# A fixed slot tile for each expert, overflow tiles, and 64 KB weight blocks whose down matrix is cut in column halves

## The reference

```python
x = x + _L0_ffn_ref(_layernorm(x), ...)        # twice
# NUM_EXPERTS = 160, TOP_K = 8, HIDDEN = 128, INTER = 64, T = 4096 tokens
probs = jax.nn.sigmoid(x @ router_w.T + expert_bias[None, :])
top_w, top_idx = jax.lax.top_k(probs, TOP_K)
top_w = top_w / (jnp.sum(top_w, axis=-1, keepdims=True) + 1e-09) * ROUTED_SCALE
h1 = jax.nn.silu(jnp.einsum('th,eih->eti', x, w_gate))
routed = jnp.einsum('eti,ehi->th', h1 * combine.T[:, :, None], w_down)   # combine: top_w at top_idx
shared = jax.nn.silu(x @ w_gate_shared.T) @ w_down_shared.T
```

## Time and profile before

| | |
|---|---|
| time, median of 3 runs | 2897.25 us (2891.38 to 2900.32) |
| the profiled execution, its own time | 2902.76 us, its span 2900.9 us |
| mean granted TensorE clock | 0.723 of full speed |
| busy: PE, DVE, ACT, POOL | 1753.3, 1334.2, 970.8, 1057.4 us |
| expert stages, about | 447 to 930 us (run 0) and 1319 to 1801 us (run 1) |

### The profile page before, as it was taken

How to read it: one execution, slowest core, us unless ns; L and a number is a source line. 1 busy time by engine, 2 the same in 40 slices (tenths; PEclk the granted TensorE clock), 3 DMA queues, 4 the chain that set the end, 5 groups by cost and what they waited for, 6 DMA issues and landing times.

```text
span 2900.9 us, 44112 instructions
## 1 busy us (share of the span) xinstructions
PE 1753.3 (60%) x13716; PEld 1146.8 (40%) x13716; DVE 1334.2 (46%) x3558; ACT 970.8 (33%) x1719; POOL 1057.4 (36%) x1177
## 2 busy tenths in 40 slices
PE   3765506776666454556776676422325488888975
PEld 2544404555444242244554454100124234455443
DVE  3648811222334677473222333543215466666644
ACT  3651102232223321312232222356761123444342
POOL 2001777724651774757714651771000200000000
PEclk9985557778878655557788787655555568998985
DMA  8941118999997111117999997120000000000001
GB/s 234 382 181 29 51 53 275 325 304 292 321 289 241 52 52 54 52 55 244 327 308 294 310 301 241 51 54 8 4 2 0 0 1 1 1 1 2 1 1 29
DMA packets 332506, 393.39 MB, mean 136 GB/s; under 512 B 57952, under 2 KB 222512, under 8 KB 332208
## 3 DMA queue, kind: packets, MB, share of 16 engines
q1 hardware_dynamic: 215616, 171.43, 19.0%
q10 hardware_dynamic: 83984, 153.13, 15.4%
q0 software_dynamic: 32768, 67.17, 7.7%
HBM read 242.13 MB, written 164.63 MB: 140 GB/s over the span
## 4 chain that ended last, share of the span: by engine, by line
PE 36%; DVE 15%; DMA 13%; ACT 11%; issue 10%; SPq 9%; POOL 6%; DVEq 0%; ACTq 0%; POOLq 0%
DMA arena<-expert_blocks 12%; SPq L1819 6%; ACT arena L955 5%; PE psum L1918 4%; PE psum L1909 4%; POOL slot_rows L1725 4%; PE psum L448 3%; SPq L1815 3%; PE psum L1347 2%; PE psum L1900 2%; PE psum L1328 2%; PE psum L432 2%; PE psum L993 1%; PE psum L427 1%; ACT arena L1210 1%
## 5 line engine op out<-in xcount | busy, mean ns | idle before, releaser
L1736 POOL DMA_INDIRECT arena<-slot_results,SLOTS x512 | 490.7, 958 | 503.1 <-DMA slot_results<-arena 285.8
L1725 POOL DMA_INDIRECT slot_rows<-arena,SLOTS x512 | 493.4, 964 | 309.4 <-issue 308.8
L1699 DVE COPY arena<-psum 128x512 f32<-128x512 f32 x288 | 198.6, 690 | 742.3 <-PE psum L1918 719.4
L1909 PE MATMUL psum<-arena 128*64 128x128 f32 x2304 | 236.5, 336 | 278.4 <-DMA arena<-expert_blocks 271.0
L1779 ACT ACTIVATE arena<-psum 128x512 f32<-128x512 f32 x288 | 171.9, 597 | 476.4 <-PE psum L1900 467.6
L1909 PEld LDWEIGHTS psum<-arena 128*64 128x64 f32 x2304 | 154.5, 165 | 349.0 <-issue 291.5
L169 POOL TENSOR_SCALAR rstd<-mv 128x4 f32<-128x4 f32 x32 | 6.2, 193 | 772.3 <-DVE mv L577 771.8
L1900 PE MATMUL psum<-ident,arena 128*128 128x128 f32 x1152 | 231.6, 335 | 84.9 <-DMA arena<-slot_rows 84.3
L1918 PE MATMUL psum<-arena 64*128 64x128 f32 x2304 | 253.3, 350 | 0.0
L1786 ACT ACTIVATE arena<-psum 128x256 f32<-128x256 f32 x288 | 110.4, 383 | 338.5 <-PE psum L1909 335.3
L1918 PEld LDWEIGHTS psum<-arena 64*128 64x128 f32 x2304 | 189.6, 230 | 64.4 <-issue 64.2
(11 more groups left out here) (234 smaller groups left out, 3064.5 us busy)
## 6 DMA issues: line engine op xcount, KB each, us to landing
arena<-expert_blocks SPq DMA_DIRECT2D x1152, 96.0 KB
arena<-slot_rows ACTq DMA_DIRECT2D x288, 256.0 KB
slot_results<-arena ACTq DMA_DIRECT2D x288, 256.0 KB
slot_rows<-zeros SPq DMA_DIRECT2D x2, 18432.0 KB, 84.2
slot_rows<-arena,SLOTS POOLq DMA_INDIRECT x512, 2.2
arena<-slot_results,SLOTS POOLq DMA_INDIRECT x512
expert_blocks<-in_expert_w SPq DMA_DIRECT2D x1, 7680.0 KB, 26.0
expert_blocks<-in_expert_w SPq DMA_DIRECT2D x1, 5120.0 KB, 52.7
```

The source lines that it names most:

```text
L1699: dve.tensor_copy(YSB[:, p].rearrange("p (c h) d -> p h c d", h=2), psum[:, first:first + 2, 0:256].rearrange("p h (c d) -> p h c d", c=2) ...
L1725: pool.indirect_dma_start(out=slot_rows[h], out_offset=bass.IndirectOffsetOnAxis(ap=SLOTS[:, t, k:k + 1], axis=0), in_=XNH[:, t], in_offse ...
L1736: pool.indirect_dma_start(out=GATHERED[:, t % TPI, k], out_offset=None, in_=slot_results[h], in_offset=bass.IndirectOffsetOnAxis(ap=SLOTS[ ...
L1909: mm = pe.matmul(psum[lo:lo + INTER, 2 + 5 * (p % 2), o:o + P], EWB[:, p, q, 0:INTER], XSBT[:, p, P * q:P * q + P], start=True, stop=True, ...
```

## The change

- **Slot tiles.** Tile e of the 288 now belongs to expert e for its first 128 tokens; the other 128 tiles take what is over, sorted by expert (`DELTA`, `MORE_GROUPS` = 32 groups). The 40 groups of own tiles (`OWN_GROUPS`) have experts that are known when the kernel is written, and the two kinds are interleaved (`GROUP_ORDER`).
- **Placing.** `FIRST` is replaced by the constant `OWN`. `rows_of_slots` takes four token tiles together: it compares with the end of the own tile, adds `DELTA` where a number is past it, runs one sum over 640 numbers so that the eight numbers of a token come out in order, multiplies by `MASK`, takes four times the eight largest and subtracts neighbours.
- **Weights.** A block is 64 KB: 128 partitions x 128 numbers. The down matrix's first 64 output columns lie in partitions 0 to 63 and the others in 64 to 127. `expert_blocks` is laid out by partition, so a partition's row is 80 KB long and holds all experts. For an own group SP issues four DMAs, each with 32 partitions and rows of 2 KB (four experts side by side); for an overflow group four DMAs with rows of 512 B, by expert numbers that it reads as before. SP's loop is written out.
- **Down products.** The gated rows of a slot tile stand in one partition half, but half of its down matrix in the other. DVE copies them across (`in_both_halves`, two copies of 64 x 256), and PE makes eight products of 64 columns where it made four of 128; the last four wait for the copies.

```diff
-        EW = INTER + D
+        OWN_GROUPS = NE // GROUP
+        MORE_GROUPS = GROUPS - OWN_GROUPS
+        GROUP_ORDER = sorted(range(GROUPS), key=lambda n: (n + 0.5) / OWN_GROUPS if n < OWN_GROUPS else (n - OWN_GROUPS + 0.5) / MORE_GROUPS)
+        EW = INTER + D // 2
-        expert_blocks = nc.dram_tensor("expert_blocks", (NE * P, EW), F32).ap()
+        expert_blocks = nc.dram_tensor("expert_blocks", (P, NE * EW), F32).ap()
...
-            dve.wait_ge(s_slotm.sem, s_slotm.at(run, t))
-            stand(dve)
-            dve.max(S8[:, j], SLOTM[:, j]).then_inc(s_s8.sem, 1)
...
+            dve.tensor_tensor(OVER, SLOTM, every(OWN_END), ALU.is_gt).then_inc(link.sem, link.one())
+            dve.wait_ge(link.sem, link.so_far())
+            dve.tensor_tensor(OVER, OVER, every(DELTA), ALU.mult).then_inc(link.sem, link.one())
+            dve.wait_ge(link.sem, link.so_far())
+            dve.tensor_tensor(OVER, SLOTM, OVER, ALU.add).then_inc(link.sem, link.one())
+            dve.wait_ge(link.sem, link.so_far())
+            stand(dve)
+            dve.tensor_tensor_scan(PLACED.rearrange("p t e -> p (t e)"), ones_row[:, 0:1].broadcast_to([P, TPI * NE]), OVER.rearrange("p t e -> p (t e)"),
+                                   0.0, ALU.mult, ALU.add).then_inc(link.sem, link.one())
+            dve.wait_ge(link.sem, link.so_far())
+            dve.tensor_tensor(PLACED, PLACED, MASK[:, TPI * i:TPI * i + TPI, :], ALU.mult).then_inc(link.sem, link.one())
+            for j in range(TPI):
+                last = TOPK * (TPI - 1 - j)
+                dve.max(S8[:, last:last + TOPK], PLACED[:, j]).then_inc(link.sem, link.one())
...
+        def in_both_halves(dve, run, h, g):
+            hr = HALVES * run + h
+            dve.wait_ge(c_he.sem, c_he.at(hr, 0, g + 1))
+            dve.tensor_copy(HEB[INTER:, g % 2, 2:4], HEB[0:INTER, g % 2, 0:2]).then_inc(c_both.sem, 1)
+            dve.tensor_copy(HEB[0:INTER, g % 2, 2:4], HEB[INTER:, g % 2, 0:2]).then_inc(c_both.sem, 1)
...
+            def own_weights(n, p):
+                for part in range(GROUP):
+                    rows = slice(P // GROUP * part, P // GROUP * (part + 1))
+                    sp.dma_start(EWB[rows, p].rearrange("p q c -> p (q c)"), expert_blocks[rows, GROUP * EW * n:GROUP * EW * (n + 1)]).then_inc(c_ew[p].sem, 16)
+            def more_weights(n, p):
...
-                    sp.dma_start(EWB[:, p, q], expert_blocks[bass.ds(e * P, P), :]).then_inc(c_ew[p].sem, 16)
+                    sp.dma_start(EWB[:, p, q], expert_blocks[:, bass.ds(e * EW, EW)]).then_inc(c_ew[p].sem, 16)
...
-            pe.wait_ge(o_link.sem, o_link.at(run, h))
-            pe.matmul(psum[:, 7, 0:NE], ident[:], FIRST, start=True, stop=True, skip_group_check=True)
+            pe.wait_ge(o_own, 3)
+            pe.matmul(psum[:, 7, 0:NE], ident[:], OWN, start=True, stop=True, skip_group_check=True)
...
-                for q in range(GROUP):
-                    c, lo = P * (q // 2), INTER * (q % 2)
-                    mm = pe.matmul(psum[:, 3 + 2 * (p % 2) + q % 2, c:c + P], HEB[lo:lo + INTER, p % 2, c:c + P],
-                                   EWB[lo:lo + INTER, p, q, INTER:EW], start=True, stop=True, skip_group_check=True, tile_position=(lo, 0))
+                for other in range(2):
+                    if other:
+                        pe.wait_ge(c_both.sem, c_both.at(hr, g, 2 * p + 2))
+                    for c in range(GROUP // 2):
+                        for half in range(2):
+                            q, lo = 2 * c + (half ^ other), INTER * half
+                            mm = pe.matmul(psum[:, 3 + 2 * (p % 2) + half, INTER * q:INTER * q + D // 2], HEB[lo:lo + INTER, p % 2, 2 * other + c],
+                                           EWB[lo:lo + INTER, p, q, INTER:], start=True, stop=True, skip_group_check=True, tile_position=(lo, 0))
...
             for run in range(HALVES):
+                in_both_halves(dve, run, 0, 0)
                 for g in range(GROUPS):
+                    if g + 1 < GROUPS:
+                        in_both_halves(dve, run, 0, g + 1)
                     results_out(dve, run, 0, g)
...
-            sp.dma_start(block_of[:, 0:INTER], whole[:, 0:INTER]).then_inc(blocked, 16)
-            sp.dma_start(block_of[:, INTER:, 0:INTER], whole[:, INTER:, 0:INTER]).then_inc(blocked, 16)
-            sp.dma_start(block_of[:, INTER:, INTER:], whole[:, 0:INTER, INTER:]).then_inc(blocked, 16)
+            sp.dma_start(block_of[:, :, 0:INTER], whole[:, :, 0:INTER]).then_inc(blocked, 16)
+            for half in range(2):
+                sp.dma_start(block_of[INTER * half:INTER * half + INTER, :, INTER:], whole[0:INTER, :, INTER + D // 2 * half:INTER + D // 2 * (half + 1)]).then_inc(blocked, 16)
```

More of the change, by code:

```diff
@@ L1493, in program @@
         INCL = view([P, NE])
-        FIRST = view([P, NE])
+        OWN_END = view([P, NE])
+        OWN = view([P, NE])
+        DELTA = view([P, NE])
+        OVER = view([P, TPI, NE])
+        PLACED = view([P, TPI, NE])
         JUNK2 = view([P, GROUP, NE], BF16)
@@ L1687, in rows_of_slots @@
[L1687 to L1691 removed]
+            link = Order(s_slot, run, i)
@@ new lines, in rows_of_slots @@
+            every = lambda row: row.unsqueeze(1).broadcast_to([P, TPI, NE])
+            dve.wait_ge(s_slotm.sem, s_slotm.at(run, TPI * i + TPI - 1))
+            dve.tensor_tensor(OVER, SLOTM, every(OWN_END), ALU.is_gt).then_inc(link.sem, link.one())
[3 more added lines that the diff above has]
+            dve.tensor_tensor(OVER, SLOTM, OVER, ALU.add).then_inc(link.sem, link.one())
@@ new lines, in rows_of_slots @@
+            stand(dve)
+            for j in range(TPI):
+                last = TOPK * (TPI - 1 - j)
+                dve.max(S8[:, last:last + TOPK], PLACED[:, j]).then_inc(link.sem, link.one())
+            dve.wait_ge(link.sem, link.so_far())
+            dve.scalar_tensor_tensor(SLOT[:].rearrange("p t k -> p (t k)"), S8[:, 0:TPI * TOPK], -1.0, S8[:, 1:TPI * TOPK + 1],
+                                     ALU.add, ALU.subtract).then_inc(link.sem, link.one())
+            dve.wait_ge(link.sem, link.so_far())
@@ L1812, in experts_sync @@
             hr = HALVES * run + h
[L1814 removed]
+            def own_weights(n, p):
[3 more added lines that the diff above has]
+            def more_weights(n, p):
+                stand(sp)
                 _, experts = nc.values_load_multi_w_load_instructions(
[L1816 removed]
+                    EXPERT[0:1, h, n, :], engines=[sp.engine], min_val=0, max_val=NE - 1,
                     skip_runtime_bounds_check_because="EXPERT counts at most NE experts and is clamped to NE - 1 where it is made")
                 for q, e in zip(range(GROUP), experts):
[L1819 removed]
+                    sp.dma_start(EWB[:, p, q], expert_blocks[:, bass.ds(e * EW, EW)]).then_inc(c_ew[p].sem, 16)
             sp.wait_ge(o_expert.sem, o_expert.at(run, h))
[L1822 to L1831 removed]
+            for g in range(GROUPS):
+                n, p = GROUP_ORDER[g], g % UNROLL
+                if hr or g >= UNROLL:
+                    sp.wait_ge(c_y.sem, c_y.at(hr, 0, g - UNROLL + 1))
+                if n < OWN_GROUPS:
+                    own_weights(n, p)
+                else:
+                    more_weights(n - OWN_GROUPS, p)
         LOGITS = (6, 2)
@@ L1947, in middle_vector @@
             dve.memset(C9[:], 0.0)
+            dve.memset(S8[:], 0.0)
+            own_tiles(dve)
             for h in range(HALVES):
```

88 lines of the change are left out of this document (47 added, 41 removed).

## The result

The change takes 3136.04 us (median of 4 runs, 3123.36 to 3145.66) against 2894.32 us for the kernel before on the same chip: the ratio is 1.083, 95% interval 1.079 to 1.088. It is slower by 8%, where 2823 us was forecast with a range of 2780 to 2905. The execution shown here took 3138.0 us, 235.2 us more than the one of before.

A forecast was written before the change was run, and what follows sets the result against it. The DMA engines were taken to bound the expert stages beside POOL, with SP as close without it. From 2902.8 us, minus 118 for weights plus 44 for placing gave 2829, less 5.5 for the median: 2823 us, range 2780 to 2905.

The forecast's parts named there:

- TensorE at the full clock fits under the first and sets the second: Expert stages: TensorE's 2.47 us a group fits under DMA's 2.81 beside POOL and sets the pace without POOL (DMA 2.35).
- rival 1: Expert stages: TensorE bounds at half clock; with the clock mix as granted 3.09 and 2.79 us a group, 2884 us; chance 0.14.
- The weights' price: Expert-stage weight DMAs: 0.91 us a group against 1.32, 0.41 us less, 118 us less over 288 groups.
- The overflow rows: Weight DMAs of an overflow group: 512 rows of 512 B cost 0.99 us, between 0.88 and 1.32.
- the own rows: Weight DMAs of an own group: 128 rows of 2 KB cost 0.85 us, between 0.72 and 1.43.
- The placing: Added DVE passes in `rows_of_slots`: 6.1 us a call, 16 calls, 44 us in sum on the path.
- the calls under the dispatch: Placing calls before the first expert stage, after the first call, lying under POOL's dispatch: they cost nothing.
- the calls between the stages: Placing calls between the first and second expert stage: 6.1, 12.8 and 18.3 us on the path.
- Rival 2: Own groups' weight loads: 32-partition DMAs pay double, 1.43 us; 25 us saved, placing's 44 stay, 2916 us; chance 0.12.
- Rival 3: Weight loads: 512 B rows, blocks 80 KB apart, cost what 768 B cost; 1.06 us a group, 2865 us; chance 0.10.
- Rival 4: Expert stages: DVE's copies hold up POOL, its pace 1.26 us becoming 1.78; 2946 us; chance 0.06.

The follow-up runs named there:

- wide_again: The changed kernel with each down product streaming 128 columns instead of 64, the extra results unread; 2890.25 us, ratio 0.998 to the kernel before.
- wide96: The changed kernel with each down product streaming 96 columns instead of 64; 2932.49 us, ratio 1.012 to the kernel before.
- half_columns: The kernel before with its four down products cut to 64 columns, leaving out half of the output; 2903.31 us, ratio 1.002.
- small_blocks: The kernel before with 64 KB blocks laid out by partition, copies across and eight 128-column down products, slots and placing as before; 2880.18 us, ratio 0.995.
- parity_again: The changed kernel without split or copies: four 128-column products, own groups 64 KB a DMA packed by parity, overflow groups 96 KB; 2908.75 us, ratio 1.004.
- wide_spread: The changed kernel with 128-column down products and the eight adds of `sum_rows` two a group instead of eight at each fourth; 2893.51 us, ratio 0.999.
- the alone-run: The kernel before plus only the change's added placing passes, on tiles that nothing reads; 2939.9 us, ratio 1.014.
- parity_span: parity_again with an own group loaded by one DMA over 128 partitions instead of four over 32 each; 2910.0 us, ratio 1.005.

## Why the prediction was wrong

**The step that failed** is the one that let TensorE pass: "TensorE at the full clock fits under the first and sets the second", and in rival 1 the condition "if the clock stays as granted". The prediction priced TensorE at 2.47 us a group at the full clock and 4.40 at half; measured are 2.21 and 4.00, both a tenth less. It then took for the forecast that the full clock holds, and for rival 1 that the mix stays as granted (0.77, 0.87), which gave 2884 us and a chance of 0.14. No case had a clock that falls because of the change. It fell to 0.50, and 4.00 us against 3.35 and 3.34 before (483.0 and 481.1 us over 144 groups) is the 192 us that the stages lost. The argument against rival 1, that it would be the busy engine then, was the wrong one: busy for 106.00 of 106.00 us it stayed low. `wide_again`, `wide96` and `half_columns` show that the columns streamed behind each weight load decide it in this loop, in both directions. Whether the columns of each pass count, or those streamed over a stretch of time, no run separates.

**The weights' price nearly held.** SP's queue in the changed kernel, 500 to 580 us:

```profile
q1 hardware_dynamic: 7303, 5.25, 25.0%
...
arena<-expert_blocks SPq DMA_DIRECT2D x81, 64.0 KB
```

That is 0.250 x 80 / 20.25 = 0.99 us a group, against 0.91 forecast and 1.32 before: a saving of 0.33 us a group and not 0.41. The overflow rows were priced a little too high (0.92 us in `small_blocks` against 0.99), so by the mean of 0.99 the own rows cost (72 x 0.99 - 32 x 0.92) / 40 = 1.05 us, an estimate, against 0.85. `parity_again` gives less for them: 33.2% of 80 us without 11.25 overflow groups at 1.32 leaves 0.84 us for each of its 14 own groups, so their price stays open between the two. With the clock up (`wide_again`: 32.1% with 104 DMAs, or 0.99) the two stages save 32.6 and 47.0 us, 80 in all where 118 were forecast; and that execution took 2871.31 us, 19 less than the median of its kernel, so 80 is rather too much. Groups there take 3.13 and 3.01 us, not 2.8 and 2.5. What holds them at that is not settled; it is not the length of DVE's sums (`wide_spread`). TensorE still waits 77.4 and 74.9 us for weights in the two stages (132.7 and 138.3 before), while SP waits 93.6 and 83.1 us for TensorE to free one of the four weight buffers (50.2 and 50.7 before). That the four buffers are too few is a rival that no run tested.

**The placing held in its sum, but partly by luck.** 44 us were forecast and the alone-run gives 41. A call in the changed kernel (DVE, start and us):

```profile
277.47 0.82 DVE L1704 TENSOR_TENSOR arena<-arena 128x640 f32<-128x640 f32 x1
...
280.16 1.49 DVE L1711 TENSOR_TENSOR_SCAN arena<-ones_row,arena 128x640 f32<-128x640 f32 x1
281.69 0.82 DVE L1714 TENSOR_TENSOR arena<-arena 128x640 f32<-128x640 f32 x1
282.66 1.01 DVE L1719 MAX8 S<-arena 128x8 f32<-128x160 f32 x4
```

The pieces are nearly as priced (4 x 0.825, 1.6, 1.0), and the first dispatch begins at 285.77, 5.3 us later instead of 6.1. But the stage begins 15.0 later: POOL took (457.10 - 285.77) - (442.05 - 280.46) = 9.7 us more for its first 128 starts, and a term for that was missing: the prediction put the calls under the dispatch at nothing. 21 of these 128 DMAs stand beside DVE passes over 640 numbers and take 1.07 to 2.13 us, together 10.4 us more than at 0.96 us each; before, four did, for 0.7 us (rows in the last section). In the alone-run the same stage begins 16.7 us later where 6.1 were forecast, the calls between the stages cost 33.6 where 37.2 were, and the two stages are 9.3 us shorter than before, for which nothing was forecast. The sum is right since these errors cancel.

**Rival 2** (32-partition DMAs at double price) fell: `parity_span` and `parity_again` differ by 0.1%. The Trainium skill's rule that partitions 0 to 31 reach half of the ports ("SBUF — State Buffer", Door 1: The DMA port swizzle) is not contradicted by that, since other transfers to all partitions ran beside; no run here shows it alone. **Rival 3** (512 B rows at the price of 768 B) fell: it needs 1.32 us for a group of 512 B rows 80 KB apart, and `small_blocks`, where all groups are such, measures 0.92. (The changed kernel's 0.99 alone would not decide it, since it lies halfway between the forecast's 0.91 and the rival's 1.06.) **Rival 4** (copies hold up POOL) fell for the copies: with them POOL makes 84 DMAs in 106 us in the changed kernel's first window as against 83. It holds in a small way for the placing passes, which the prediction had not considered there.

## What to carry to other kernels

When an edit splits TensorE's passes, price the new loop at both clock levels and ask whether it still fits under the next limit at the lower one; a granted clock read before the edit is no property of the stretch and may fall with it. Few streamed columns behind each weight load is the sign to look for, and streaming columns that nobody needs can be the faster choice (3133 to 2890 us here, which only brings the time back to that of before). Where two limits are as close as DMA and SP here, an edit that relieves one is worth only the distance to the other.

## What the runs showed of the hardware

- TensorE, busy without a pause, stayed at 1.2 GHz (0.50) from 480 to 742 us and in most of the rest of stages of 574 and 582 us with passes of 64 columns, and came back to 2.4 GHz only at the starts of three halves, for less than 12 us each; the same weight loads with 96 columns were granted 0.89 and 0.74, with 128 columns 0.98 and 0.90, in the same windows.
- A pass of 64 columns is hardly shorter than one of 128 when each has its own load of 128 weight columns: 2.21 against 2.27 us a group of 16 such passes (and 12 others) at the full clock.
- GpSimd's indirect DMAs grow while DVE makes passes over 640 fp32 numbers from and to SBUF. Beside the placing call of 287.80 to 294 us two of them take 1.35 and 1.27 us instead of 0.96, and over the dispatch 21 of 128 such cost 10.4 us:

```profile
288.56 0.96 POOL L1776 DMA_INDIRECT slot_rows<-arena,SLOTS  x1 [0.30 <-issue]
289.82 1.35 POOL L1776 DMA_INDIRECT slot_rows<-arena,SLOTS  x1 [0.30 <-issue]
291.48 1.27 POOL L1776 DMA_INDIRECT slot_rows<-arena,SLOTS  x1 [0.31 <-issue]
```
